# Batch 1's head products in two-tile pieces, and P.V products in runs of two key tiles

## The reference, cut to what matters

```python
q = _rms(heads(wq), qn_w); k = _rms(heads(wk), kn_w); v = heads(wv)
scores = jnp.einsum('bhqd,bhkd->bhqk', q, k) * HD ** (-0.5)
attn = jax.nn.softmax(jnp.where(causal, scores, -jnp.inf), axis=-1)
ao = jnp.einsum('bhqk,bhkd->bhqd', attn, v) ...
```

## Time and profile before

| what | value |
|---|---|
| median of 3 runs | 1404.76 us (1403.76 to 1405.98) |
| the profiled execution's own time | 1405.97 us |
| its span, first to last instruction | 1404.2 us |
| busy: PE, DVE, ACT, POOL | 1298.0, 1075.4, 765.6, 327.0 us |
| slots 0 to 8 of layer 0's attention and training | about 37 to 599 us of the span |

### The profile page before, as it was taken

How to read it: one execution, slowest core, us unless ns; L and a number is a source line. 1 busy time by engine, 2 the same in 40 slices (tenths; PEclk the granted TensorE clock), 3 DMA queues, 4 the chain that set the end, 5 groups by cost and what they waited for, 6 DMA issues and landing times. The chain is left out here.

```text
span 1404.2 us, 26518 instructions
## 1 busy us (share of the span) xinstructions
PE 1298.0 (92%) x8834; PEld 992.0 (71%) x8834; DVE 1075.4 (77%) x3354; ACT 765.6 (55%) x1657; POOL 327.0 (23%) x458
## 2 busy tenths in 40 slices
PE   4789999999999999979986899899999999999997
PEld 2666767677777777655654677678888888888776
DVE  6888888889898988463247876687777887787776
ACT  6344546455555464634333565566666666666664
POOL 3101111110101010100006166433321233333264
PEclk9699999999999999989997999999999999999999
DMA  2000000000000000010000320202221012220012
GB/s 103 1 1 1 1 1 1 1 1 1 1 1 1 1 1 1 1 46 0 0 0 4 87 71 28 69 1 61 61 61 43 28 53 61 61 61 9 9 33 59
DMA packets 39698, 36.21 MB, mean 26 GB/s; under 512 B 2320, under 2 KB 38160, under 8 KB 39312
## 3 DMA queue, kind: packets, MB, share of 16 engines
q1 hardware_dynamic: 37520, 30.36, 7.2%
q0 software_dynamic: 2048, 4.20, 1.0%
HBM read 26.17 MB, written 8.39 MB: 25 GB/s over the span
## 5 line engine op out<-in xcount | busy, mean ns | idle before, releaser
L1137 ACT ACTIVATE pe_<-PS 128x512 f32<-128x512 f32 (+3 forms) x384 | 175.9, 488 | 140.0 <-PE PS L2196 136.0
L1895 DVE CUSTOM_DVE_ANT_0 PS<-PS,mask_row 128x128 f32<-128x128 f32 (+7 forms) x256 | 194.0, 765 | 49.5 <-PE PS L2346 47.4
L1205 ACT ACTIVATE PN<-PS,NM 128x128 f32<-128x128 f32 (+7 forms) x256 | 189.2, 740 | 76.2 <-DVE NM L1895 44.7
L2353 PE MATMUL PS<-ident,PN 128*128 128x128 f32 x1152 | 176.4, 276 | 11.6 <-DVE pe_ L1903 7.4
L2345 PE MATMUL PS<-KA,QA 128*128 128x512 f32 (+3 forms) x384 | 158.2, 413 | 17.6 <-issue 7.4
L2353 PEld LDWEIGHTS PS<-ident,PN 128*128 128x128 f32 x1152 | 135.6, 141 | 49.5 <-issue 30.2
L2176 PE MATMUL PS<-kta,qta 128*128 128x512 f32 (+3 forms) x384 | 149.7, 416 | 6.3 <-DVE tmqs L1571 2.3
L2196 PE MATMUL PS<-qtb,kta 128*128 128x512 f32 (+3 forms) x384 | 134.1, 388 | 0.9 <-ACT pe_ L1137 0.9
L2346 PE MATMUL PS<-KB,QA 128*128 128x512 f32 (+3 forms) x384 | 129.8, 351 | 0.0
L1571 DVE CUSTOM_DVE_ANT_0 PS<-PS,W 128x128 f32<-128x128 f32 (+3 forms) x256 | 125.0, 495 | 4.7 <-PE PS L2176 3.3
L907 POOL TENSOR_SCALAR_AFFINE_SELECT pe_<-pe_ 128x512 f32<-128x512 f32 x64 | 42.0, 657 | 362.7 <-ACT pe_ L1137 362.7
(11 more groups left out here) (314 smaller groups left out, 2910.5 us busy)
## 6 DMA issues: line engine op xcount, KB each, us to landing
W<-w SPq DMA_DIRECT2D x40, 384.0 KB, 4.1
W<-by_expert SPq DMA_DIRECT2D x10, 256.0 KB, 4.7
expert_out<-YS SPq DMA_DIRECT2D x10, 256.0 KB, 2.3
by_expert<-WOZ SPq DMA_DIRECT2D x2, 1024.0 KB, 6.8
W<-w SPq DMA_DIRECT2D x1, 1728.0 KB, 9.7
W<-w SPq DMA_DIRECT2D x1, 1536.0 KB, 6.0
X<-x SPq DMA_DIRECT2D x2, 512.0 KB, 4.8
out<-X SPq DMA_DIRECT2D x2, 512.0 KB, 3.2
```

Source lines behind the costliest of these rows:

```text
L1137: act.activation(pe_[:, h, n % 2, 0:w], PS[:, 4 + h % 2, 0:w], ACT.Exp, scale=HD0 ** -0.5)\
L1205: act.activation(prob_rows(u, r), scores_of(u), ACT.Exp, bias=NM[:, u:u + 1], scale=-1.0, accum_out=SM[:, r % 2, u:u + 1]).then_inc(score_ ...
L1895: dve.tensor_tensor_reduce(scores_of(u), scores_of(u), mask_row[:, S - w:S], -HD1 ** -0.5, -MASKED, ALU.add, ALU.min, NM[:, u:u + 1]).then ...
L2353: ins = pe.transpose(PS[:, ring_bank[item, r], (j - 4 * k) * P:(j - 4 * k + 1) * P], prob_rows(u, r)[:, j * P:(j + 1) * P], ident[:, :])
```

## The change

- Batch 1's sums move from before slot 0 into slot 0 (items a4 and a10), its roots too (ACT, at a16, written straight into `inv1`). Reciprocals and `by_inverse` are done in slot 1, `by_weights` and half of `low` in slot 2, the rest of `low` in slot 3, each in pieces of two tiles (sums: four) ahead of listed `a` items. `high` is four pieces on ACT in slot 2.
- The copies of the first trip's keys and queries on POOL go in two halves, each after its own half of `low`; PE's first turns wait for halves. A memset of `grc` moves from DVE to POOL.
- `pv` takes two neighbouring pairs n at once, six runs in place of twelve, at the places of the odd ones of before (pv1, pv3, ...); in SLOT and SLOT_TAIL six letters s go, so that what followed an even `pv` moves up into its place.
- The exponentials have three buffers: the third is the part of W0 that holds the first mixture's weights, whose load (1728 KB) moves from the start to the end of the slots, ahead of W1's loads on the same queue.

```diff
+        NPV = NB // 2
+        LAST = [1, NPV - 1]
+        def prob0(n):
+            if n % 3 < 2:
+                return pe_[:, :, n % 3, :]
+            return W0[:, W0_FIRST:W0_FIRST + HG * 512].rearrange("p (h n) -> p h n", h=HG)
+        LATE_ROOT = 16
+        LATE_DVE = {(0, 4): ("sums", 0), (0, 10): ("sums", 1), (1, 4): ("inverse", 0), (1, 9): ("scale", 0), (1, 14): ("inverse", 1), (1, 19): ("scale", 1),
+                    (1, 24): ("inverse", 2), (1, 29): ("scale", 2), (1, 34): ("inverse", 3), (1, 39): ("scale", 3),
+                    (2, 2): ("by_qn", 0), (2, 7): ("by_kn", 0), (2, 12): ("by_qn", 1), (2, 17): ("by_kn", 1),
+                    (2, 22): ("by_qn", 2), (2, 27): ("by_kn", 2), (2, 32): ("by_qn", 3), (2, 37): ("by_kn", 3),
+                    (2, 42): ("low", 0), (2, 46): ("low", 1), (3, 2): ("low", 2), (3, 7): ("low", 3)}
+        LATE_ACT = {(2, 22): 0, (2, 30): 1, (2, 38): 2, (2, 45): 3}
-        for n in range(NB + 1):
-            if n < NB:
-                SECOND0 += [("st", n, h) for h in range(HG)]
-            if n >= 1:
-                SECOND0 += [("pv", n - 1)]
+        for n in range(NB):
+            SECOND0 += [("st", n, h) for h in range(HG)]
+            if n >= 2 and n % 2 == 0:
+                SECOND0 += [("pv", n // 2 - 1)]
...
-            sp.dma_start(W0[:, W0_FIRST:], w0_in[:, W0_FIRST:]).then_inc(mix_loaded, 16)
             sp.wait_ge(s0_dve.sem, s0_dve.at(("zt", 1), TRIPS - 1))
             sp.wait_ge(s0_pe.sem, s0_pe.at(("to", 1), TRIPS - 1))
+            sp.dma_start(W0[:, W0_FIRST:], w0_in[:, W0_FIRST:]).then_inc(mix_loaded, 16)
...
-                        if n >= 2:
-                            wait(act, s0_pe, ("pv", n - 2), before)
-                        act.activation(pe_[:, h, n % 2, 0:w], PS[:, 4 + h % 2, 0:w], ACT.Exp, scale=HD0 ** -0.5)\
+                        if n >= 3:
+                            wait(act, s0_pe, ("pv", (n - 3) // 2), before)
+                        act.activation(prob0(n)[:, h, 0:w], PS[:, 4 + h % 2, 0:w], ACT.Exp, scale=HD0 ** -0.5)\
...
+            def late_piece(kind, j):
+                inverse = inv1[:, 2 * j * 32:(2 * j + 2) * 32]
+                if kind == "sums":
+                    head_sums(1, j)
+                elif kind == "inverse":
+                    dve.wait_ge(hroot, 2 + j // 2 + 1)
+                    dve.reciprocal(inverse, inverse).then_inc(late_inverse, 1)
+                elif kind == "scale":
+                    dve.wait_ge(late_inverse, j + 1)
...
-                    if r == ("a", LATE_AT):
-                        for k in range(2):
-                            if s == 1:
-                                by_inverse(1, k)
-                            elif s == 2:
-                                by_weights(1, k)
-                            elif s == LATE_HIGH:
-                                low(1, k)
+                    if r[0] == "a" and (s, r[1]) in LATE_DVE:
+                        late_piece(*LATE_DVE[s, r[1]])
```

More of the change, by code:

```diff
@@ L331, in program @@
         SECOND0 = []
-        for n in range(NB + 1):
-            if n < NB:
-                SECOND0 += [("st", n, h) for h in range(HG)]
-            if n >= 1:
-                SECOND0 += [("pv", n - 1)]
+        for n in range(NB):
+            SECOND0 += [("st", n, h) for h in range(HG)]
+            if n >= 2 and n % 2 == 0:
+                SECOND0 += [("pv", n // 2 - 1)]
             if n == 7:
                 SECOND0 += [("to", 0)]
+        SECOND0 += [("pv", NPV - 1)]
         SECOND0 += [("to", 1)]
@@ L686, in program @@
         rms_ready, hinv = sem("rms_ready"), sem("head_inverse_ready")
+        late_inverse, late_scaled, late_normed, late_high = (
+            sem("late_inverse"), sem("late_scaled"), sem("late_normed"), sem("late_high"))
         qkv_w, qkv_ps, qkv_done, hsq, hsum, hroot, hscale, hnorm, hhi, hlo = (
@@ L719, in inverse_of, with late_tiles, late_heads @@
         def inverse_of(b, k):
-            return inv1[:, 4 * k * 32:(4 * k + 4) * 32] if b else head_quarter(hss, b, k)
+            return head_quarter(hss, b, k)
+        def late_tiles(j):
+            return slice(TB + 2 * j, TB + 2 * j + 2)
+        def late_heads(j, lo, hi):
+            return QKV[:, late_tiles(j), lo:hi].rearrange("p t (h e) -> p t h e", e=HD0)
         def head_factors(b, k):
@@ L843, in _ @@
             link(pool.memset(okay[:, :], 1.0))
+            link(pool.memset(grc[:, :, :], 0.0))
             for tm, at in ((tmk, QM), (tmv, HD0)):
@@ L883, in tokens, with half, first_keys, first_queries @@
                 ins.then_inc(t_pool.sem, 1)
+            def half(ap, k):
+                return ap[:, 4 * k:4 * k + 4, :, :]
+            def first_keys(k):
+                pool.wait_ge(hlo, k + 1)
+                pool.tensor_copy(half(put(tmk, 0), k), half(heads(QKV, 0, 0, D), k))
+                pool.tensor_copy(half(put(tmk, HD0), k), half(heads(LO, 0, 0, D), k))
+                pool.tensor_copy(half(put(tmk, 2 * HD0), k), half(heads(QKV, 0, 0, D), k)).then_inc(s0_keys, 1)
+            def first_queries(k):
+                tmq = tmqs[:, 0, :, :]
+                pool.tensor_copy(half(put(tmq, 0), k), half(heads(QKV, 0, 0, 0), k))
+                pool.tensor_copy(half(put(tmq, HD0), k), half(heads(QKV, 0, 0, 0), k))
+                pool.tensor_copy(half(put(tmq, 2 * HD0), k), half(heads(LO, 0, 0, 0), k)).then_inc(s0_queries, 1)
             def keys(trip, b, g):
@@ L899, in values @@
             def values(trip, b, g):
-                wait(pool, s0_pe, ("pv", NB - 1), trip, 1)
+                wait(pool, s0_pe, ("pv", NPV - 1), trip, 1)
                 pool.tensor_copy(put(tmv, 0), heads(QKV, b, g, 2 * D)).then_inc(s0_values, 1)
@@ L905, in diagonals @@
                     wait(pool, s0_act, ("ex", n, HG - 1), trip)
-                    block = pe_[:, :, n % 2, 0:P]
+                    block = prob0(n)[:, :, 0:P]
                     pool.affine_select(out=block, in_=block, compare_op=ALU.is_ge, fill=0.0, base=0,
@@ L917, in slot @@
                     if batch0(s + 1):
-                        pool.wait_ge(hlo, 4)
+                        pool.wait_ge(hlo, 6)
                     keys(s + 1, batch0(s + 1), group0(s + 1))
@@ L923, in slot @@
                 diagonals(before, DIAG0[4:8])
-            keys(0, batch0(0), group0(0))
-            queries(0, batch0(0), group0(0))
+            for k in range(2):
+                first_keys(k)
+                first_queries(k)
             tokens(0, 0)
@@ L1062, in root @@
                 act.wait_ge(hsum, 2 * b + k + 1)
-                act.activation(head_quarter(hsd, b, k), head_quarter(hss, b, k), ACT.Sqrt, bias=eps[:, 1:2],
+                to = inv1[:, 4 * k * 32:(4 * k + 4) * 32] if b else head_quarter(hsd, b, k)
+                act.activation(to, head_quarter(hss, b, k), ACT.Sqrt, bias=eps[:, 1:2],
                                scale=1.0 / HD0).then_inc(hroot, 1)
@@ L1091, in _ @@
             square(1, 1)
-            root(1, 0)
-            root(1, 1)
             def ttt(run):
@@ L1112, in slot @@
                 for r in order:
+                    if s == 0 and r == ("a", LATE_ROOT):
+                        root(1, 0)
+                        root(1, 1)
+                    if r[0] == "a" and (s, r[1]) in LATE_ACT:
+                        j = LATE_ACT[s, r[1]]
+                        act.wait_ge(late_normed, 2 * j + 2)
+                        act.copy(LO[:, late_tiles(j), :].bitcast(F32R), QKV[:, late_tiles(j), 0:2 * D])\
+                            .then_inc(late_high, 1)
                     if r[0] == "t" and r[2] == "kvn":
@@ L1141, in _ @@
             for s in range(1, TRIPS):
-                if s == LATE_HIGH:
-                    high(1, 0)
-                    high(1, 1)
                 slot(SLOT, s, s - 1)
@@ L1361, in _ @@
             low(0, 0)
-            head_sums(1, 0)
             low(0, 1)
-            head_sums(1, 1)
-            head_inverse(1, 0)
-            head_inverse(1, 1)
             dve.wait_ge(const_ready, N_CONST)
+            def late_piece(kind, j):
[7 more added lines that the diff above has]
+                    dve.wait_ge(late_inverse, j + 1)
+                    by = inverse.rearrange("p (t h) -> p t h", t=2).unsqueeze(3).broadcast_to([P, 2, 32, HD0])
+                    both = late_heads(j, 0, 2 * D)
+                    dve.tensor_tensor(both, both, by, ALU.mult).then_inc(late_scaled, 1)
+                elif kind == "low":
+                    dve.wait_ge(late_high, j + 1)
+                    dve.tensor_tensor(LO[:, late_tiles(j), :], QKV[:, late_tiles(j), 0:2 * D],
+                                      LO[:, late_tiles(j), :], ALU.subtract).then_inc(hlo, 1)
+                else:
+                    dve.wait_ge(late_scaled, j + 1)
+                    one = late_heads(j, 0, D) if kind == "by_qn" else late_heads(j, D, 2 * D)
+                    by = w0(kind[3:]).unsqueeze(1).unsqueeze(1).broadcast_to([P, 2, H0, HD0])
```

(21 more changed lines are left out.)

10 lines of the change are left out of this document (3 added, 7 removed).

## The result

The changed kernel takes 1428.14 us (median of 4 runs, 1427.61 to 1433.99) against 1404.38 before (4 runs by then): the ratio is 1.0182, 95% interval 1.0158 to 1.0205. The profiled execution took 1427.87, 21.9 more than the one before, with a span of 1426.1. The forecast was 1411.1 with a range of 1394 to 1419: the sign was right, the size too small, and the time lies outside the range.

A forecast was written before the change was run, and what follows sets the result against it. PE was taken as nearly full, DVE with little room, all engines on one list. Slots 1 to 3 +0.4, -1.8, -0.8, slots 4 to 7 +6.0, tail +3.5, front -1.0: +6.3, from 1404.76 to 1411.1 us (1394 to 1419).

The forecast's parts named there:

- The clean slot: Slots without batch 1's head norm, 65.56 us before: the runs of two were to lose 1.5 us a slot.
- bound of 4.2: Largest loss from the runs of two if nothing is caught up: even runs' lengths, 5.1, less 0.9 of fixed time saved.
- The tail: Part after the slots, 37.70 us before, little DVE work to catch up with: 3.5 us lost.
- The pieces: Batch 1's head norm on DVE in slots 1 to 3, costing 4.3, 3.6 and 1.2; 2.8, 2.1 and 0.8 show.
- its own rule: In slots 1 to 3, as much DVE work hides as PE runs late, 1.5 us a slot (0.4 in slot 3).
- The front: Ahead of and in slot 0: first cast 2.7 us sooner, less 1.7 for sums in slot 0, so 1.0 gained.
- Behind the slots: After the slots, third buffer and late weights' load: nothing priced; a late load would show whole, up to 9.7 us.
- C: Rival, slower still: new idle brings the half clock back into slots 1 to 7, about 1.0 a slot; 1418 us; chance 0.10.
- B: Rival, a draw: half of the losses and half of the pieces show; 1403 us; chance 0.18.
- A: Rival, faster: waits are absorbed and each run's fixed time is saved; 1384 us at the full, 1394 half; chance 0.22.
- fixed 0.15: Part of each `pv` run's time on PE not due to its columns, 0.15 us; six runs fewer save 0.9 a slot.

The follow-up runs named there:

- the last experiment: The changed kernel with `to0` put back behind y of the second chunk's sweep 1, nothing else; 1429.4 us (one run).
- `st` left in place: The changed kernel with the even `pv` places deleted where they stood, so no `st` moves up and `to0` stays behind y; 1423.5 us (1.0135).
- pieces alone: The changed kernel with single `pv` in the old order, two exponential buffers and the weights' load at the start; 1401.1 us (0.9976).
- runs alone: The kernel before with only the runs of two, third buffer, late load and new order strings; head norm's blocks stay; 1432.7 us (1.0210).
- pieces in tanh waits: Single `pv` in the old order, three buffers, batch 1's pieces put behind the sum zh of sweeps in slots 1 to 3; 1393.2 us (0.9935).

## Why the prediction was wrong

**The clean slot is the step that failed**: 1.5 lost was forecast, 3.58 came, near the bound of 4.2 that stood for "nothing caught up". By place, from how much later the training's product behind the run starts in its slot than before:

| run of pairs | product: before, after | late so far | share | forecast |
|---|---|---|---|---|
| 0, 1 | y2: 377.37, 381.28 | 0.57 | 0.57 | 0.4 |
| 2, 3 | ds4: 390.08, 394.65 | 1.23 | 0.66 | 0.15 |
| 4, 5 | dc0: 400.70, 405.69 | 1.65 | 0.42 | 0.4 |
| 6, 7 and `to0` | y2: 409.62, 415.75 | 2.79 | 1.14 | 0.3 |
| 8, 9 | zc4: 421.10, 427.82 | 3.38 | 0.59 | 0.4 |
| 10, 11 | next slot | 3.58 | 0.20 | -0.15 |

Two places hold 1.35 of the 2.1 missing. At pairs 2 and 3 I let the run fall on time that was "most of it idle before" zc4; no idle stands there. At pairs 6 and 7 I priced only `to` in the place ahead of y, and neither DVE's division behind it (0.51 by the last experiment) nor the run of two ahead of the next y (0.64 in the trace, 2.15 to 2.79). The mechanism was right: the even runs covered waits, an exponential behind a tanh (0.67 and 0.99 of idle, where about 0.9 was forecast), y1 no sooner. What was wrong was to let the lateness be caught up: of the 1.0 at pairs 4 and 5, 0.6 was to be. Between the sites, slack gave back 0.3 to 0.4 at a time at most.

**The tail**: 3.5 forecast, 5.95 measured, over its own bound of 4.2. That bound was cover lost. With `st` left in place the tail lost 2.4, within it, though its `st` waited 3.5 us for exponentials (0.9 before). The other 3.6 came with the new order, which the prediction did not price: it named the last run ahead of dc4 and its wait for the mask (0.5 here), but not what the moved-up `st` and runs do to sl and grc.

**The pieces** were priced well: 8.6 shows where nothing hides them (9.1 forecast). That 5.5 shows in the changed kernel, with 5.7 forecast, is luck in part. The prediction let as much DVE work hide as PE is late, 1.5 a slot; with the 3.58 that came, its own rule would have left about 0.7 in slot 1 and nothing in slot 2, where 1.83 and 2.98 show. The excess fell with the clock at 1.00, and no stall took the old blocks' place: PE's longest wait in slots 1 to 3 is 1.2, a little over the 1 us that the prediction allowed.

**The front** gained 4.1 in place of 1.0. The first cast came 2.95 sooner (2.7 forecast); slot 0 was 1.1 shorter, where 1.7 longer was forecast, at a granted clock of 0.92 against 0.79. At 0.79 too, the pieces alone have a slot 0 of 51.26, 0.9 longer. With the new front the first cast stood between 37.04 and 39.02 in nine profiles, with the old one at 40.00 and 39.08 in two (before and runs alone), so this term is known to some 2 us only.

**Behind the slots** 1.97 was lost where nothing was forecast. The code there is the same. PE's 5096 products are busy for 753.4 us in place of 748.4, at clocks that differ from place to place (0.83 at 620 to 630 us, just behind the slots, where before had 0.68 at 600 to 610). The stretch took 803.7 to 811.8 in the nine profiles with the late load, 805.5 and 809.1 in the two without, so no cost of the load shows. What sets where the clock falls stays open.

The terms then add up: 6.3 + 7 x 2.08 + 2.45 (tail) - 3.06 (front) - 0.2 (pieces) + 1.97 = 22.0, against the 21.9 measured.

**The rivals.** C is excluded: the clock is 1.00 in slots 1 to 7, with waits of PE of up to 1.2 (the idle of 0.5 quoted against C was 0.4 at most in PE's waits of slot 5). B let half of the losses show, 0.75 a clean slot, where 3.58 came. A had its fixed 0.15 a run right: a 512-wide run of two took 1.85 from its start (402.48) to the next product (404.33), where two single ones are 1.00 each. By the Trainium skill, "TensorEngine Tiling (Array Packing)", Key Properties, a change of the tiling mode drains the engine. The 0.15 agrees in sign, but no run shows how much of it is a drain. And a saving on PE is worth nothing where PE waits: of 63.85 busy in 65.56 us, 3.85 could go for 0.26. The Trainium skill, "Perfetto Trace Analysis", Identifying the Most-Contended Engine, says that the busy share of the matmuls is not a good measure of how close a kernel is to its roofline, because pipelined matmuls look smaller in a trace. This case adds another reason to distrust the share: PE was 97% busy, and yet its work was not what set the slot's time.

## What to carry to other kernels

Before you move a product out of a hand-written order, ask what waits where it stands and what stands where it goes: cost it by its place, not by its length, and count on no catching up along a closed chain until a trace shows the slack. Work whose result no engine must take soon (here `pv`) was a good filler for PE's waits; the one other filler tried, products whose result DVE must take soon, was none. The same holds for DVE: pieces of 0.4 to 0.7 us cost 8.6 us ahead of listed products and next to nothing in the 0.48 us in which it waits for a tanh anyway.

## What was not expected of the hardware

A DVE piece that is longer than the wait that it stands in didn't lengthen the chain: the reciprocal of 0.54 in a wait of 0.48 left zh to sl at 0.90, since neighbouring DVE instructions overlap in the trace (zh from 93.33 for 0.42, the reciprocal from 93.66). The pieces of 0.68 were expected to stick out by 0.2. In the run of the pieces in tanh waits all eight of them left zh to sl at 0.93 or 0.94, some 0.03 more than without a piece.
